# Cross attention on one core: cross scores as three fp32r products, zeros ahead of the first operands, halved first loads, finer PSUM claims, last stage by batch, a new merge

## The chip, the core and the metric

The kernel runs on one NeuronCore of a Trainium2 chip. A core has TensorE (matrix products, into the PSUM banks), VectorE, ScalarE, GpSimd and SyncE (here it only issues DMAs), each with an instruction stream of its own that runs in order; semaphores join them. The metric is the time of one execution on the device in microseconds, lower is better.

## What is computed

Two attention blocks over 8 batches of 112 tokens, width 256, 16 heads of 16. The first attends from x to the first 112 rows of a context under a causal mask and ends in a layer norm. The second is self attention, then cross attention to all 375 context rows, plus a feed-forward of width 1024 on the block's input:

```python
# block 0 (keys, values = context)
Q = relu(x @ Wq.T + bq); K = relu(ctx @ Wk.T + bk); V = relu(ctx @ Wv.T + bv)
x = layer_norm(softmax(mask(Q K^T / 4)) V + x) * gamma + beta
# block 1 (tgt = x, src = ctx)
q, k, v = split(ln1(tgt) @ sa_wqkv)
result = tgt + softmax(causal(q k^T / 16)) v @ sa_wproj + sa_bproj
k2, v2 = split(ln2(src) @ ed_wkv);  q2 = ln2(result) @ ed_wq
result = result + softmax(q2 k2^T / 16) v2 @ ed_wproj + ed_bproj
result = result + relu(ln3(tgt) @ ff_w1 + ff_b1) @ ff_w2 + ff_b2
```

## The kernel before

Batches go in four groups g of two (b = 0, 1). Heads are packed so that one product over 32 rows of the array serves two heads; four such products, for r = 0 to 3, use four row groups side by side (a "round" below). All work is cut into steps, and the steps are named by tuples: `("S", g, l, b)` is the self scores of layer l, needed only for their row maxima; `M` transposes and spreads the maxima; `X` makes the scores again, transposed and less their maximum (minus-max products with `sel`, then the scores), for ScalarE's exp; `V` sums values; `O` brings the sum back to token rows. The cross attention has the same steps: `cS` (four per batch, i = 0 to 3), `cM`, `cX` and `cV` (three chunks of 125 context rows each), `cO`; then `t2` transposes the result, `y` projects it, and the result is stored. `k2`, `v2`, `q2` are the cross projections, `cT` the transposed context; `h`, `f` the feed-forward; `q0`, `k0`, `v0`, `xT`, `q1`, `k1`, `v1`, `t1`, `proj`, `xqT` the projections and transposes of the self attention; `rows` spreads row vectors over partitions, `flag` and `general` handle fully masked rows.

The order of all steps is one string, `MIX`: each letter takes the next step of one stream (`STREAMS`), and every engine runs its part of each step in that order (`run`). TensorE writes into a ring of six PSUM banks, in three pairs. `homes` gives each job a pair, or one bank if its kind is in `SMALL`, the one filled longest ago; `claim` makes TensorE wait until the jobs that had it before have been read. A quad step (S, X, cS, cX) has two jobs, one for r = 0, 1 and one for r = 2, 3.

In `cross_scores` and `cross_shifted` the operands q2 and k2 are fp32, and each such matmul is recorded as two matmuls in the trace. The cross projections already work with split operands: an fp32 value is rounded to fp32r (HI), the rest is kept (LO), and three fp32r products, each recorded once, stand for one fp32 product:

```python
TERMS = ((HI, HI), (HI, LO), (LO, HI))
```

In the profile VectorE's reduction of cS is L1021, of S L1000, ScalarE's exp L848, its copy of k2 L901 and of q2 L829; `add_values` (V, cV) is L644, the minus-max products L619, cS L740, cX L754, X L631, S L593 and L599, most other products L493.

Of the kernel before, what the change touches and what calls it, by code (L numbers as in the profile page):

```python
# [7 lines left out]
F32 = mybir.dt.float32  # L8
# [12 lines left out]
G = 2  # L21
# [81 lines left out]
def b_steps(g, b):  # L103

    return [("cS", g, b, i) for i in range(4)] + [("cM", g, b), ("cX", g, b, 0), ("cX", g, b, 1), ("cV", g, b, 0), ("cX", g, b, 2), ("cV", g, b, 1), ("cV", g, b, 2), ("cO", g, b)]
# [9 lines left out]
           "F": [x for g in GROUPS for x in b_steps(g, 1)], "Y": [(n, g) for g in GROUPS for n in ("t2", "y")],  # L115
# [33 lines left out]
SMALL = ("counts", "M", "O", "cM", "cO", "f")  # L149
# [27 lines left out]
BEFORE = [(("rows", 0), ("v0", 0)), (("rows", 0), ("general",))]  # L177
for g_ in GROUPS:
    BEFORE += [(("keys", g_), ("v0", g_)), (("cV", g_, 0, 2), ("cV", g_, 1, 0))]
    for b_ in range(G):  # L180
        BEFORE += [(("keys", g_), ("S", g_, 0, b_)), (("masks", g_), ("M", g_, 0, b_)), (("late", g_), ("O", g_, 0, b_)), (("norm2", g_), ("f", g_, b_)), (("h", g_, 1), ("f", g_, b_)), (("f", g_, b_), ("y", g_)),
# [3 lines left out]
        if g_:  # L185
            BEFORE += [(("t2", g_ - 1), ("cO", g_, b_)), (("t1", g_ - 1), ("O", g_, 1, b_))]
# [4 lines left out]
    if g_:  # L191
        BEFORE += [(("h", g_ - 1, 1), ("xT", g_)), (("cV", g_ - 1, 1, 2), ("cV", g_, 0, 0)), (("proj", g_ - 1), ("t1", g_)), (("cT", g_ - 1, G - 1), ("stats", g_)),
                   (("t2", g_ - 1), ("t2", g_))]
# [15 lines left out]
def build(nc, xk_t_d, x_nat_d, keys_d, c_nat_d, c_t_d, c_first_d, mask_d, w_d, flat_d, mask_const_d, row_d, out_d):  # L209
    ctx = ExitStack()  # L210
    with ctx:
# [83 lines left out]
        unsplit = k2[1][:, :, :, :].rearrange("p b c s -> p (b c s)")[:, 0:C * 2 * U].rearrange("p (c u) -> p c u", c=C)  # L295
# [15 lines left out]
        PREP_DVE, PREP_LATE = 14, 2  # L311
        split_hi, split_lo = sem("weights_hi"), sem("weights_lo")
        prep_act = sem("prep_act"); prep_dve, prep_late = sem("prep_dve"), sem("prep_late"); prep_pool = sem("prep_pool")
        xk_loaded, x_loaded, stored = ([sem(f"{n}{i}") for i in range(2)] for n in ("xk_loaded", "x_loaded", "stored"))
# [7 lines left out]
        kv_loaded, qk0_loaded, v0_loaded = sem("kv_loaded"), sem("w_qk0_loaded"), sem("w_v0_loaded")  # L322
# [19 lines left out]
        a_ot = [twin("out_transposed0", 1), signal("out_transposed1", 1)]  # L342
        a_xq = twin("norm2_scaled", 2); a_q2 = twin("q2_scaled", 2); a_h = signal("hidden_biased", FF)
# [12 lines left out]
        v_res = signal("result", 1)  # L356
# [7 lines left out]
        def filled_and_taken(job):  # L364
# [7 lines left out]
                    "t1": lambda: (a_ot[0], 1), "proj": lambda: (v_proj, G), "xqT": lambda: (a_xq, 2), "q2": lambda: (a_q2, 2),  # L372
                    "h": lambda: (a_h, 4 * i[0] + 4), "cT": lambda: (v_ct, i[0] + 1), "k2": lambda: (a_k2, C * (i[0] + 1)), "shift": lambda: (a_shift, 2),
                    "v2": lambda: (v_v2, i[0] + 1), "cS": lambda: (x_max[i[0]], 2 * i[1] + i[2] + 1),
                    "cM": lambda: (c_m[i[0]], 1), "cX": lambda: (c_exp[i[0]], 2 * i[1] + i[2] + 1),
                    "cO": lambda: (x_o[i[0]], 2), "t2": lambda: (a_ot[1], 1), "y": lambda: (v_res, 1)}[kind]()
# [918 lines left out]
```

## Time and profile before

| | |
|---|---|
| three runs | 386.32, 382.94, 385.3 us (median 385.3) |
| the profiled execution | 384.1 us, span from first to last instruction 382.3 us |
| mean granted clock of TensorE | 0.995 |
| TensorE busy with matmuls | 341.8 us (89%), 4144 records |
| VectorE, ScalarE, GpSimd busy | 226.6, 172.5, 53.2 us |
| DMA | 13.43 MB, mean 35 GB/s |

The busy time of an engine is the union of its instructions. PE is TensorE's matmuls, PEld its weight loads, which run beside them; DVE is VectorE, ACT ScalarE, POOL GpSimd, SPq the DMA issues of SyncE. The difference between the execution's time and its span, 1.8 us, lies around the instructions.

### The profile page before, as it was taken

To read this page: it belongs to the slowest core of one execution; us is meant where nothing else is said; L and a number is where in the kernel's file an instruction comes from. 1 tells how busy PE (TensorE), PEld (TensorE's weight loads), DVE (VectorE), ACT (ScalarE), POOL (GpSimd) and SP (SyncE) were. 2 spreads that over 40 slices of the span, in tenths; PEclk is the share of its full clock that TensorE was granted. 3 is DMA by queue.
4 is the path that set the end of the run, shared out by engine and by line. 5 is a ranking of instruction groups with operands and counts; after the bars stand their busy time and mean duration, and the time that the engine had idled before them with its cause. 6 is when DMAs were issued, how large, how long until landed. Compare 5 with 4: busy or idle time off the path is not lost.

```text
span 382.3 us, 9700 instructions
## 1 busy us (share of the span) xinstructions
PE 341.8 (89%) x4144; PEld 261.7 (68%) x4144; DVE 226.6 (59%) x558; ACT 172.5 (45%) x297; POOL 53.2 (14%) x67
## 2 busy tenths in 40 slices
PE   7888699998999999998999999879989989887894
PEld 4666589886867777766668777655968757575663
DVE  5398997746657639564487545838943263645212
ACT  3346654465570263914326144655464535211551
POOL 2014141041320010120211012240100211000000
PEclk9999989999999999999999999999999999999999
DMA  7684103000000100000000020000000000000001
GB/s 223 186 328 137 63 2 104 3 2 2 25 2 0 45 40 24 3 2 2 24 6 3 0 82 2 3 0 26 3 2 2 2 2 2 3 0 0 3 2 48
DMA packets 4260, 13.43 MB, mean 35 GB/s; under 512 B 525, under 2 KB 1669, under 8 KB 3962
## 3 DMA queue, kind: packets, MB, share of 16 engines
q1 hardware_dynamic: 3928, 12.72, 10.0%
q8 instruction: 33, 0.54, 0.6%
q10 hardware_dynamic: 290, 0.10, 0.1%
q14 instruction: 9, 0.07, 0.1%
HBM read 11.89 MB, written 0.92 MB: 34 GB/s over the span
## 4 chain that ended last, share of the span: by engine, by line
PE 69%; DVE 16%; ACT 8%; issue 6%; ACTq 0%; DVEq 0%
PE ring L493 34%; PE ring L740 7%; DVE negmax L1021 7%; ACT exps L848 6%; PE ring L754 4%; PE ring L619 4%; PE ring L599 4%; PE ring L593 3%; PE acc L644 3%; PE ring L631 3%; DVE negmax L1000 3%; PE ring L663 2%; PE ring L611 1%; PE ring L705 1%; PE ring L525 1%
## 5 line engine op out<-in xcount | busy, mean ns | idle before, releaser
L1021 DVE TENSOR_REDUCE negmax<-ring 112x2 f32<-112x750 f32 x64 | 57.1, 936 | 42.2 <-PE ring L740 42.1
L848 ACT ACTIVATE exps<-ring 125x896 f32<-125x896 f32 x48 | 41.4, 914 | 43.7 <-PE ring L754 43.5
L1232 POOL TENSOR_SCALAR_AFFINE_SELECT exps<-exps 112x896 f32<-112x896 f32 x32 | 31.4, 1007 | 130.9 <-ACT exps L848 130.9
L1000 DVE TENSOR_REDUCE negmax<-ring 112x8 f32<-112x896 f32 x32 | 33.4, 1086 | 17.9 <-PE ring L599 17.7
L644 PE MATMUL acc<-exps,v 125*17 125x112 f32 (+1 forms) x1280 | 39.4, 264 | 0.8 <-ACT v L825 0.4
L644 PEld LDWEIGHTS acc<-exps,v 125*17 125x17 f32 (+1 forms) x1280 | 28.7, 98 | 13.8 <-issue 10.2
L848 ACT ACTIVATE exps<-ring,pad 112x896 f32<-112x896 f32 x32 | 30.5, 1004 | 16.7 <-PE ring L631 16.7
L740 PE MATMUL ring<-k,q 32*112 32x376 f32 x256 | 28.8, 517 | 10.2 <-DVE negmax L1021 6.0
L493 PE MATMUL ring<-w_b,h 128*112 128x256 f32 x128 | 29.5, 383 | 0.0
L619 PE MATMUL ring<-maxrows,sel 32*125 32x224 f32 (+1 forms) x320 | 19.1, 310 | 10.8 <-issue 2.9
L882 ACT ACTIVATE h<-ring,flat_c 128x224 f32<-128x224 f32 x32 | 11.7, 449 | 34.4 <-PE ring L493 34.4
L619 PEld LDWEIGHTS ring<-maxrows,sel 32*125 32x125 f32 (+1 forms) x320 | 12.3, 175 | 21.2 <-issue 13.7
L493 PEld LDWEIGHTS ring<-w_b,h 128*112 128x112 f32 x128 | 22.0, 177 | 6.6 <-issue 1.4
L493 PE MATMUL ring<-n,w_b 128*128 128x224 f32 x128 | 26.0, 357 | 0.1
L493 PEld LDWEIGHTS ring<-n,w_b 128*128 128x128 f32 x128 | 23.6, 190 | 1.6 <-issue 1.3
L740 PEld LDWEIGHTS ring<-k,q 32*112 32x112 f32 x256 | 9.9, 169 | 19.4 <-issue 19.1
L754 PE MATMUL ring<-q,k 32*125 32x224 f32 x384 | 22.7, 349 | 0.0
L493 PE MATMUL ring<-n,w_a 128*128 128x224 f32 x96 | 20.3, 360 | 0.2 <-ACT n L804 0.2
L493 PE MATMUL ring<-ct,wkv 128*128 128x376 f32 x96 | 18.4, 341 | 0.8 <-issue 0.7
L1217 POOL TENSOR_TENSOR rstd<-var_e,half 112x1 f32<-112x1 f32 x16 | 9.6, 603 | 67.8 <-DVE var_e L1113 51.2
L493 PEld LDWEIGHTS ring<-wkv,ct 128*125 128x125 f32 x144 | 17.6, 186 | 2.1 <-DVE negmax L1021 1.1
L493 PE MATMUL ring<-wkv,ct 128*125 128x256 f32 x144 | 19.1, 286 | 0.0
(143 smaller groups left out, 552.1 us busy)
## 6 DMA issues: line engine op xcount, KB each, us to landing
c_nat<-in_ctx SPq DMA_DIRECT2D x4, 750.0 KB
w_b<-in_w_b SPq DMA_DIRECT2D x1, 2304.0 KB, 10.2
xk_t<-in_xk_t SPq DMA_DIRECT2D x4, 448.0 KB, 4.1
w_a<-in_w_a SPq DMA_DIRECT2D x1, 1280.0 KB, 5.7
xh<-in_keys SPq DMA_DIRECT2D x4, 224.0 KB, 2.8
x_nat<-in_x SPq DMA_DIRECT2D x4, 224.0 KB, 4.0
out<-x SPq DMA_DIRECT2D x4, 224.0 KB, 2.4
w_qk<-in_w_qk SPq DMA_DIRECT2D x1, 512.0 KB, 4.7
```

Of the source, the lines that this page charges most:

```text
L493: m = nc.tensor.matmul(dst, lhs, rhs, start=start and n == 0, stop=n == len(pairs) - 1, skip_group_check=True)
L593: nc.tensor.matmul(bank[r][0:T, 0:4 * T], add_mask[:, l, slot(g, b), :], ident_b[:, :].unsqueeze(1).to_broadcast([T, 4, T]), start=True, s ...
L599: m = nc.tensor.matmul(bank[r][0:T, j * T:(j + 1) * T], qf[g % 2][32 * r:32 * r + 32, c, b, e, :], kf[g % 2][32 * r:32 * r + 32, c, b, :], ...
L619: nc.tensor.matmul(bank[r][0:k, 2 * c * T:2 * (c + 1) * T], sel[rows, c:c + 1].to_broadcast([32, k]), maxrows[i][rows, :], start=c == 0, s ...
L644: m = nc.tensor.matmul(acc[s][32 * p:32 * p + VW, 2 * c + m_, 0:T], vals(8 * c + 2 * r + e), exps[0:k, EXP_AT[job], rr, j * T:(j + 1) * T] ...
L740: m = nc.tensor.matmul(bank[r][0:T, 0:SP], q2[g % 2][rows, c, b, e, :], k2[g % 2][rows, b, c, :], start=True, stop=True)
L754: m = nc.tensor.matmul(bank[r][0:CH, 2 * c * T:2 * (c + 1) * T], k2[g % 2][rows, b, c, ch * CH:(ch + 1) * CH], q2[g % 2][rows, c, b, :, :] ...
L848: return nc.scalar.activation(exps[0:k, EXP_AT[job], :, :], o[0:k, :, 0:4 * T], ACT.Exp, bias=bias)
L882: a_h.step(nc.scalar.activation(h[g % 2][:, 4 * i0 + i, :, :].rearrange("p b t -> p (b t)"), o[:, i // 2, (i % 2) * G * T:(i % 2 + 1) * G ...
L1000: v_max[b].step(nc.vector.tensor_reduce(negmax[0][:, slot(g, b), 2 * m_:2 * m_ + 2, :], o[0:T, :, 0:4 * T].rearrange("p r (j t) -> p r j t ...
L1021: x_max[b].step(nc.vector.tensor_reduce(negmax[1][:, b, 2 * m_:2 * m_ + 2, i], o[0:T, :, 0:S], AX.X, ALU.max, negate=True), g, 2 * i + m_ + 1)
L1232: p_masked[b].step(nc.gpsimd.affine_select(e, e, [[0, 8], [1, T]], ALU.is_ge, 0.0, base=0, channel_multiplier=-1), g, k)
```

## The change

1. q2 and k2 are kept in two parts, HI and LO, as fp32r. ScalarE writes HI as it wrote the whole before; VectorE then computes the rest from the PSUM bank (`key2_rest`, `query2_rest`). cS and cX run the three `TERMS` instead of one fp32 product. cS and the release of k2's and q2's banks wait for VectorE.
2. `keep_busy`: TensorE multiplies zeros, ten bf16 products of 128x512, before its first step.
3. x's and the context's features, and the weights of q0 and k0, come by two loads each, with semaphores of their own; q0 waits for its own half.
4. `quad` claims its second pair of banks when it gets to r = 2. Masks and S wait for fewer of the mask steps.
5. `t2` and `y` go by batch, each in one bank, so do the copy, the residual add and the store; they belong to the streams B and F.
6. A new string `MIX`. `unsplit` (the cross weights as loaded) lies over h[1] instead of k2[1], and the DMA scratch is set to 1024.

```diff
-SMALL = ("counts", "M", "O", "cM", "cO", "f")
+SMALL = ("counts", "M", "O", "cM", "cO", "f", "t2", "y")
...
-MIX = ("RRLAANLNCNEDECDNCPAJCWNCWDEPIWDJINDPIJCIPDCDPIAJPAAIAJHJCJIHDEPCDPCEPEDCIDCDPJEAJIPAJAHAPINAAFIFJBPIJBKBABEPCHBNEBABPFBF"
+MIX = ("RALARLNNDENCAECDCNPJCNWCWDPIWDJICPDCJEIDNPDJPJAIAJAPDIJPHICHDCIAEPCEPEDPEIDPJCDCJIAJAIAPPAPAHFNIBHBBJBIJFKEBFEBAEPBBFABB"
...
-        q2 = [sb(f"q2_{i}", [128, C, G, 2, T]) for i in range(2)]
+        q2 = [sb(f"q2_{i}", [128, 2, C, G, 2, T], F32R) for i in range(2)]
...
-        k2 = [sb(f"k2_{i}", [128, G, C, SP]) for i in range(2)]
+        k2 = [sb(f"k2_{i}", [128, 2, G, C, SP], F32R) for i in range(2)]
...
-            load_x(0)
-            sp.dma_start(w_qk0[:, :, :, :].rearrange("p s c u -> p (s c u)"), w_d["qk0"]).then_inc(qk0_loaded, 16)
-            sp.wait_ge(xk_loaded[0], 16)
+            for part in range(2):
+                load_x(0, part)
+                sp.dma_start(w_qk0[:, part, :, :].rearrange("p c u -> p (c u)"), w_d["qk0"][:, part * C * U:(part + 1) * C * U]).then_inc((q0_loaded, k0_loaded)[part], 16)
+            sp.wait_ge(xq_loaded[0], 16)
...
-                pair = [claim(pe, step + (m,)) for m in range(2)]
-                return [pair[r // 2][:, r % 2, :] for r in range(R)]
+                pairs = {}
+
+                def bank(r):
+                    if r // 2 not in pairs:
+                        pairs[r // 2] = claim(pe, step + (r // 2,))
+                    return pairs[r // 2][:, r % 2, :]
+                return bank
...
-                pe.wait_ge(*a_q2.done(g))
-                pe.wait_ge(*a_k2.at(g, C * (b + 1)))
+                pe.wait_ge(*v_q2.done(g))
+                pe.wait_ge(*v_k2.at(g, C * (b + 1)))
                 bank = quad(("cS", g, b, i))
-                for r in range(R):
-                    rows = slice(32 * r, 32 * r + 32)
-                    m = nc.tensor.matmul(bank[r][0:T, 0:SP], q2[g % 2][rows, c, b, e, :], k2[g % 2][rows, b, c, :], start=True, stop=True)
-                    if r % 2:
-                        end(m)
+                for n, (qp, kp) in enumerate(TERMS):
+                    for r in range(R):
+                        rows = slice(32 * r, 32 * r + 32)
+                        m = nc.tensor.matmul(bank(r)[0:T, 0:SP], q2[g % 2][rows, qp, c, b, e, :], k2[g % 2][rows, kp, b, c, :], start=n == 0, stop=n == 2, skip_group_check=True)
+                        if n == 2 and r % 2:
+                            end(m)
...
+            def keep_busy(n):
+
+                for _ in range(n):
+                    nc.tensor.matmul(ring[2][:, 1, :], idle.bitcast(BF16)[:, 0:128], idle.bitcast(BF16), start=True, stop=True, skip_group_check=True)
+
+            pe.wait_ge(prep_dve, 1)
+            keep_busy(10)
...
+            def key2_rest(g, b):
+                o = is_filled(dve, ("k2", g, b))
+                dve.wait_ge(*a_k2.at(g, C * (b + 1)))
+                for i in range(C):
+                    hi, lo = (k2[g % 2][:, part, b, i, :] for part in (HI, LO))
+                    v_k2.step(nc.vector.scalar_tensor_tensor(lo, o[:, i, 0:SP], shift_k[:, i:i + 1], hi.bitcast(F32), ALU.add, ALU.subtract), g, C * b + i + 1)
+
+            def query2_rest(g):
+                o = is_filled(dve, ("q2", g))[:, :, 0:G * T].rearrange("p c (b t) -> p c b t", b=G)
+                dve.wait_ge(*a_q2.done(g))
+                for e in range(2):
+                    hi, lo = (q2[g % 2][:, part, :, :, e, :] for part in (HI, LO))
+                    v_q2.step(nc.vector.scalar_tensor_tensor(lo, o, eo_scale[:, 1, e:e + 1], hi.bitcast(F32), ALU.mult, ALU.subtract), g, e + 1)
```

How the order changes is shown at three places, all on TensorE. A row is a line of the kernel, what it writes and reads, the shape of the output and the number of matmuls as written (an fp32 one is two records in the trace).

The first is the start, up to the first self scores. Before, with rows (L560 to the second L493), flag (L569), q0 and k0 (L493, eight), masks, S (L593, L599):

```order
L560 MATMUL ring<-exps,ones_row 125x256
L562 MATMUL ring<-exps,ones_row 112x512
L563 MATMUL ring<-exps,ones_row 112x256
L493 MATMUL ring<-exps,ones_row 112x256 x2
L569 MATMUL acc<-ones,first_masked 1x1
L493 MATMUL ring<-xk_t,w_qk 128x224 x8
```

And after, with the zeros in the first row (L818):

```order
L818 MATMUL ring<-acc_sb 128x512 x10
L578 MATMUL ring<-exps,ones_row 125x256
L504 MATMUL ring<-xk_t,w_qk 128x224 x4
L587 MATMUL acc<-ones,first_masked 1x1
L504 MATMUL ring<-xk_t,w_qk 128x224 x4
L580 MATMUL ring<-exps,ones_row 112x512
L581 MATMUL ring<-exps,ones_row 112x256
L504 MATMUL ring<-exps,ones_row 112x256 x2
```

q0 moved ahead of the flag, and the second part of rows behind k0.

The second is the last cross key projection (k2(3,1), L504 with ct and wkv) and what follows it, after; before, it stands far ahead of its first cS:

```order
L504 MATMUL ring<-ct,wkv 128x376 x12
L637 MATMUL ring<-maxrows,sel 125x224 x8
L774 MATMUL ring<-q_1,k_1 125x224 x24
L759 MATMUL ring<-k_1,q_1 112x376 x24
L662 MATMUL acc<-exps,v_1 17x112 x16
```

One cX (L637, L774) stands between k2(3,1) and the two cS that read it (L759).

The third is the end, from the last cX on. Before:

```order
L619 MATMUL ring<-maxrows,sel 125x224 x8
L754 MATMUL ring<-q_1,k_1 125x224 x8
L644 MATMUL acc<-exps,v_1 17x112 x32
L663 MATMUL ring<-flat_c,acc_sb 112x128 x4
L493 MATMUL ring<-w_b,o_t 112x256 x4
L525 MATMUL ring<-flat_c,o_nat 128x112 x4
L493 MATMUL ring<-w_b,o_t 112x256 x4
```

And after:

```order
L637 MATMUL ring<-maxrows,sel 125x224 x8
L774 MATMUL ring<-q_1,k_1 125x224 x24
L662 MATMUL acc<-exps,v_1 17x112 x16
L801 MATMUL ring<-flat_c,o_nat 128x112 x2
L662 MATMUL acc<-exps,v_1 17x112 x16
L681 MATMUL ring<-flat_c,acc_sb 112x128 x4
L504 MATMUL ring<-w_b,o_t 112x256 x2
L801 MATMUL ring<-flat_c,o_nat 128x112 x2
L504 MATMUL ring<-w_b,o_t 112x256 x2
```

The y of group 2 is gone from between cO (L663, now L681) and the transposes (L525, now L801), and t2 and y of batch 0 of group 3 stand ahead of those of batch 1.

## Rows read from the trace of the kernel before

**Rows 1.** The page, part 1: busy time of TensorE (PE) and the others.

```profile
PE 341.8 (89%) x4144; PEld 261.7 (68%) x4144; DVE 226.6 (59%) x558; ACT 172.5 (45%) x297; POOL 53.2 (14%) x67
```

**Rows 2.** Stretches: from:to, length, busy us of PE, PEld, DVE, ACT, POOL, then clock.

```profile
0.00:20.00 20.00, 16.11 (x86) 11.64 (x90) 9.10 (x40) 7.26 (x15) 2.08 (x7) 1.00 0.66 201
40.00:50.00 10.00, 7.07 (x114) 5.43 (x110) 9.21 (x27) 5.42 (x11) 2.88 (x4) 0.85 0.09 23
50.00:350.00 300.00, 277.17 (x3341) 214.57 (x3334) 182.55 (x427) 137.47 (x239) 42.08 (x51) 1.00 0.04 13
350.00:380.00 30.00, 24.05 (x382) 17.16 (x380) 7.54 (x14) 10.95 (x15) 0.00 (x0) 1.00 0.03 9
```

**Rows 3.** The page, part 4: the chain that ended last.

```profile
PE 69%; DVE 16%; ACT 8%; issue 6%; ACTq 0%; DVEq 0%
```

**Rows 4.** Timeline of the start (start us, length us, engine, line, tiles, idle before).

```profile
3.37 1.91 PE L562 MATMUL ring<-exps,ones_row 1*112 1x512 f32 x2
...
5.99 0.31 SPq L419 DMA_DIRECT2D x_nat<-in_x  x1
...
7.88 1.02 ACT L811 ACTIVATE rows_sb<-ring 112x1024 f32<-112x1024 f32 x1 [0.35 <-PE ring L493]
7.94 5.71 PE L493 MATMUL ring<-xk_t,w_qk 128*128 128x224 f32 x16
...
14.67 0.94 PE L593 MATMUL ring<-mask_c,add_mask 112*112 112x448 bf16 x4 [0.97 <-ACT kf L804]
```

**Rows 5.** Groups of products in 57.4 to 60 us (count, busy us, mean ns).

```profile
L493 PE MATMUL ring<-n,w_a 128*128 128x224 f32 x15 | 3.0, 353 | 0.0
```

**Rows 6.** Timeline of TensorE from 47 to 50.5 us.

```profile
47.08 1.76 PE L631 MATMUL ring<-qf,kf 32*112 32x224 f32 x16
48.77 1.70 PE L644 MATMUL acc<-exps,v 112*17 112x112 f32 x32
```

**Rows 7.** Timeline of TensorE: a cS step and the step behind it.

```profile
190.88 0.90 PE L740 MATMUL ring<-k,q 32*112 32x376 f32 x8 [0.22 <-DVE negmax L1021]
191.72 0.54 PE L663 MATMUL ring<-flat_c,acc_sb 128*112 128x128 f32 x3
```

**Rows 8.** Timeline from 191.47 to 191.7 us: only the cS step's second round runs.

```profile
191.26 0.52 PE L740 MATMUL ring<-k,q 32*112 32x376 f32 x4
```

**Rows 9.** Timeline from 357.565 to 357.6 us: two rounds run.

```profile
357.36 0.31 PE L619 MATMUL ring<-maxrows,sel 32*125 32x224 f32 x4
357.48 0.39 PE L754 MATMUL ring<-q,k 32*125 32x224 f32 x4
```

**Rows 10.** Timeline of TensorE: a cX step and the step behind it.

```profile
353.17 0.96 PE L754 MATMUL ring<-q,k 32*125 32x224 f32 x16
354.06 0.96 PE L644 MATMUL acc<-exps,v 125*17 125x112 f32 x32
```

**Rows 11.** Timeline of TensorE: fp32r products over the whole array.

```profile
76.19 2.37 PE L493 MATMUL ring<-wkv,ct 128*125 128x256 f32 x18
78.49 0.47 PE L619 MATMUL ring<-maxrows,sel 32*112 32x224 f32 x8
```

**Rows 12.** VectorE's nearest form (count, busy us, mean ns, idle before).

```profile
L1164 DVE SCALAR_TENSOR_TENSOR wkv<-k,flat_c,wkv 128x512 fp32r<-128x512 f32 x2 | 1.5, 742 | 0.0
```

**Rows 13.** Weight loads of the cX products (count, busy us, mean ns).

```profile
L754 PEld LDWEIGHTS ring<-q,k 32*125 32x125 f32 x384 | 16.7, 183 | 0.0
```

**Rows 14.** Timeline of the end.

```profile
373.83 1.89 PE L493 MATMUL ring<-w_b,o_t 128*112 128x256 f32 x8
374.33 0.42 DVE L1095 TENSOR_TENSOR o_nat<-ring,sums 112x256 f32<-112x256 f32 x1
...
375.56 0.55 PE L525 MATMUL ring<-flat_c,o_nat 112*128 112x112 f32 x4
...
376.74 1.98 PE L493 MATMUL ring<-w_b,o_t 128*112 128x256 f32 x8 [0.64 <-ACT o_t L869]
378.76 0.69 DVE L1160 TENSOR_TENSOR x<-ring,x 112x512 f32<-112x512 f32 x1 [2.31 <-PE ring L493]
```

More of the change, by code:

```diff
@@ L618, in minus_max @@
                         rows = slice(32 * r, 32 * r + 32)
-                        nc.tensor.matmul(bank[r][0:k, 2 * c * T:2 * (c + 1) * T], sel[rows, c:c + 1].to_broadcast([32, k]), maxrows[i][rows, :], start=c == 0, stop=False, skip_group_check=True)
+                        nc.tensor.matmul(bank(r)[0:k, 2 * c * T:2 * (c + 1) * T], sel[rows, c:c + 1].to_broadcast([32, k]), maxrows[i][rows, :], start=c == 0, stop=False, skip_group_check=True)
             def self_max_rows(g, l, b):
@@ L751, in cross_shifted @@
                 for c in range(C):
-                    for r in range(R):
-                        rows = slice(32 * r, 32 * r + 32)
-                        m = nc.tensor.matmul(bank[r][0:CH, 2 * c * T:2 * (c + 1) * T], k2[g % 2][rows, b, c, ch * CH:(ch + 1) * CH],
-                                             q2[g % 2][rows, c, b, :, :].rearrange("p e t -> p (e t)"), start=False, stop=True, skip_group_check=True)
-                        if c == C - 1 and r % 2:
-                            end(m)
+                    for n, (qp, kp) in enumerate(TERMS):
+                        for r in range(R):
+                            rows = slice(32 * r, 32 * r + 32)
+                            m = nc.tensor.matmul(bank(r)[0:CH, 2 * c * T:2 * (c + 1) * T], k2[g % 2][rows, kp, b, c, ch * CH:(ch + 1) * CH],
+                                                 q2[g % 2][rows, qp, c, b, :, :].rearrange("p e t -> p (e t)"), start=False, stop=n == 2, skip_group_check=True)
+                            if c == C - 1 and n == 2 and r % 2:
+                                end(m)
             def cross_sum(g, b, ch):
@@ L775, in cross_out, with out2_transposed @@
                 tokens_first(o, RING["cO", g, b])
-            def out2_transposed(g):
-                rows_transposed(("t2", g), o_nat[1], lambda b: pe.wait_ge(*x_o[b].done(g)))
+            def out2_transposed(g, b):
+                o = claim(pe, ("t2", g, b))
+                pe.wait_ge(*x_o[b].done(g))
+                for c in range(C):
+                    m = nc.tensor.transpose(o[:, 0, c * T:(c + 1) * T], o_nat[1][:, b, c * 128:(c + 1) * 128], ident[0:T, 0:T])
+                end(m)
             def hidden_out(g, b):
@@ L1154, in add_hidden, with result @@
                 v_f[b].step(nc.vector.tensor_tensor(x1[g % 2][:, b, :], o[0:T, 0, 0:U], x1[g % 2][:, b, :], ALU.add), g, 1)
-            def result(g):
-                o = is_filled(dve, ("y", g))
-                for b in range(G):
-                    dve.wait_ge(*v_f[b].done(g))
-                v_res.step(nc.vector.tensor_tensor(x1[g % 2][:, :, :], o[0:T, :, 0:U], x1[g % 2][:, :, :], ALU.add), g, 1)
+            def result(g, b):
+                o = is_filled(dve, ("y", g, b))
+                dve.wait_ge(*v_f[b].done(g))
+                v_res[b].step(nc.vector.tensor_tensor(x1[g % 2][:, b, :], o[0:T, 0, 0:U], x1[g % 2][:, b, :], ALU.add), g, 1)
             def weights_lo(i):
```

118 lines of the change are left out of this document (66 added, 52 removed).

## The prediction

> **What bounds the kernel now.** I read the page's busy times first: TensorE has matmuls in flight for 341.8 of 382.3 us, VectorE works 226.6, ScalarE 172.5 [rows 1]. Then the same by stretch: TensorE lacks 3.9 us in the first 20, 2.9 in 40 to 50, 22.8 in the 300 us from 50 to 350, and 6.0 in the last 30 [rows 2]. The reader is to see that the middle is nearly full, and that holes of several per cent stand only at both ends and around 45 us. The chain that ended last says the same: 69% TensorE, 16% VectorE, 8% ScalarE, 6% issue [rows 3]. So work taken off TensorE counts nearly in full, work added to VectorE counts only where TensorE has nothing else queued, and the ends are read by timeline.
>
> **The sum** is made against the profiled execution, 384.1 us (span 382.3). The median of three runs is 385.3, so 384.1 stands 0.3% below it; a forecast from it may be low by 1.2. About 1% is what a measurement of this kernel can tell from no change.
>
> **Cross scores in three fp32r products.** There are 32 steps cS and 24 steps cX. A cS step is recorded as 8 matmuls, in two rounds of four that run side by side on four row groups. It starts at 190.88, its second round at 191.26, the next step at 191.72: 0.84 us [rows 7, 8]. Whole-array fp32 matmuls of 224 columns stand 3.0/15 = 0.20, nearer 0.19 without the last one's drain, apart [rows 5]; by columns that is 0.32 for 376, so 0.84 is two rounds of 0.32 and 0.20 of starting and handing over. A cX step has four rounds of 0.19 and 0.13 on top: 353.17 to 354.06, 0.89 [rows 10]. Afterwards cS has three rounds and cX six, each of single-record matmuls. What does such a round cost? Eighteen fp32r products of 256 columns over the whole array take 76.19 to 78.49, 2.30, less the same 0.20 for the handing over 0.117 each [rows 11]: 0.17 for 376 columns. For 224 columns on row groups, the second fp32r round of the minus-max products and the first behind it stand 0.12 apart in rounded figures [rows 9]; 256 columns cost 0.117, so I take 0.11. cS: 3 x 0.17 + 0.20 = 0.71, 0.13 less, x32 = -4.2. cX: 6 x 0.11 + 0.13 = 0.79, 0.10 less, x24 = -2.4. **Together -6.6.** Lower end: a fp32r round costs half a fp32 one (0.16 and 0.095), 0.16 and 0.19 less a step, -9.7. Upper end: no round is shorter than the weight load recorded for it, 0.183 [rows 13]; cS 0.75 and cX 1.23, -2.9 and +8.2, +5.3. I take the inner value because those 0.12 and 0.117 are such rounds, weight loads included.
>
> The Trainium skill (TensorE: Matmul & The Clock Gate, Part 3, Packing small matmuls) says that a weight load overlaps a matmul in flight only when it is for another row group, and its section on LDWEIGHTS prices a load at P/1.2 ns, 104 ns for the 125 columns of cX. By that rule cX would go, as an estimate, from 4 x (104 + 187) to 6 x (104 + 93) ns, no gain, and cS from 2 x (93 + 313) to 3 x (93 + 157) ns; the sum would be some 5 us later. The trace speaks against it: eighteen products that each load all rows anew stand 0.117 apart [rows 11], where load and product one after the other would be 0.21.
>
> **The rests on VectorE.** Splitting k2 adds 16 scalar_tensor_tensor of 376 columns, q2 adds 8 of 448. The nearest row is 742 ns for 512 columns [rows 12]; by columns 0.55 and 0.65, 8.8 + 5.2 = 14.0 us. Two instructions each make twelve groups that stand in VectorE's queue with ScalarE's copy ahead of them. They hold a pair of banks 1.1 or 1.3 us longer, and cS waits for them instead of for ScalarE; behind them in VectorE's queue are the maxima that free the ring. Where other work lies between k2 and its first cS this is hidden. In the new order it isn't for the last one, k2(3,1), which has one cX between (0.79 and its minus-max products), about as long as ScalarE's copy: VectorE's 1.1 us are bare. I take two such places of twelve, **+2.5**; the ends are 0 and 14.0.
>
> **The start.** Before, the one-row products fill 3.37 to 7.8, q0 and k0 take 7.94 to 13.65, and the first S begins at 14.67 [rows 4]. q0 and k0 run there at 5.71/16 = 0.357 a matmul against 0.20 later [rows 4, 5]: TensorE is at the lower of its two levels (1.2 against 2.4 GHz), though one-row products had kept it busy for over 4 us. (The profile's clock column has 1.00 for the first 20 us [rows 2]; I go by the products.) Afterwards ten zero products of 512 columns come first: at the lower level 0.357 x 512/448 = 0.41 each, from about 1.2 us to 5.3. rows(0) takes half of the 1.91 of rows 4, to 6.2; q0's operands are there by 5.99 even unhalved (the load that waits for the second one is issued then); q0 1.5 at the upper level, to 7.7; the flag still waits for its own chain until 7.8; k0 to 9.4; rows(1), 4.5 before, 2.3 at the upper level, to 11.7. ScalarE's copy of rows(1), 1.02, frees the second pair of S at 12.7, while the finer claim lets the first pair start at 11.7. So 14.67 becomes 11.7 to 12.7, **-2.3**. The halving is worth nothing here, because the flag holds k0; if the flag's cover goes, q0's earlier operands would be worth up to 1.5. Ends: +0 (the zeros don't raise the clock) and -3.5.
>
> The page of the skill named above (Part 1) says that the array is throttled by default and that activity releases it. The trace agrees in the pair 0.357 and 0.20, but the busy one-row stretch did not release it, so busy time alone isn't it; all-zero products are shown by no run here.
>
> **The dip at 47 us.** The granted clock of 40 to 50 is 0.85; the X step's second half at 47.08 takes 1.76 and the one behind it 1.70, where such steps take 0.96 [rows 2, 6, 10]: 1.5 us. Ahead of them TensorE idles most of its 2.9 us. The new merge puts v0(1), 1.7 us of products, among these steps, and k2(0,0) ahead of the V. I take **-1.0** of the 1.5; ends 0 and -2.5.
>
> **The end.** In the last 9 us: y(2) of both batches stands between the cross output and its transposes, which start at 375.56 although o_nat is ready at 374.75 (0.8); then transposes 0.55, copy, y 1.98 for both batches, result 0.69, store [rows 14]. By batch, half of each remains: transposes 0.3, y 1.1, result 0.45, and y(3,0) fits into the wait ahead. 0.8 + 0.25 + 0.9 + 0.25 and 0.1 on ScalarE's copy: **-2.3**; ends -1.5 and -3.0. Splitting all eight t2 and y adds about 0.2 to an instruction on ScalarE and VectorE, hidden in the middle. Twice as many stores and first loads cost SyncE issue time, with nobody waiting for it.
>
> **The new merge otherwise: 0.** It can only move the 22.8 us of holes. Thin covers are there in both orders: t1 straight behind the last O, cO behind its cV. A quarter of the holes either way is 5.7.
>
> **Sum:** 384.1 - 6.6 + 2.5 - 2.3 - 1.0 - 2.3 = **374.4**.
>
> **Rivals.**
> (a) The merge closes a quarter of the middle's holes: 368.7. For it: banks come in smaller pieces, t2 and y take one bank each, a quad claims its second pair later. Against: k2 and q2 hold theirs longer.
> (b) It opens as much: 380.1. For it: steps cS stand in twos and threes in the order with two maxima each on VectorE, which holds 16% of the chain [rows 3].
> (c) The zeros don't raise the clock, and the start stays as it was: 376.7.
> (d) VectorE's rests all lie on the path: 14.0 for 2.5, 385.9. For it: they queue ahead of maxima. Against: VectorE idles 155 us.
> (e) Slower than before: weight loads bound the short rounds. Every row-group round costs 0.183 [rows 13], so that cX gets 0.34 longer: +5.3 for -6.6, 386.3. The point is a round of 0.174 in both steps, where the whole change comes to nothing. This is the place of the rule of the skill quoted above (weight loads hidden only behind other row groups). Against it stand the 0.12 and 0.117.
>
> **Chances.** Forecast 0.48, (a) 0.17, (b) 0.12, (c) 0.08, (d) 0.09, (e) 0.06. The range goes from 367 to 384: it leaves out (d), (e) and a deeper (a), 0.2. Faster by over 1% (below 381.4) holds the forecast, (a), (c) and most of (b): 0.82. Within 1%: 0.14. Slower: 0.04.
>
> **What would show it.** cS to the next step 0.71 and cX 0.79 when nothing waits; 24 more VectorE instructions, 14 us; q0's and k0's matmuls 0.19 to 0.2 apart, the first S at 11.7 to 12.7; a clock of 1.00 in 40 to 50; from the y product ahead of the last transposes to the end of the span 6.2 us instead of 8.5 (373.83 to 382.3). The prediction fails if rounds of row groups stand over 0.15 apart, if TensorE's waits for k2's and q2's rests exceed 5 us, or if its idle time between 50 and 350 us changes by over 6.

## The result, and the profile after

The changed kernel takes 375.06 us (median of four runs, 370.83 to 377.79) against 385.77 for the one before: a ratio of 0.966, 95% interval 0.956 to 0.976. Medians are over all runs, but each ratio here and below leaves out the runs in a second, slower state with a lower granted clock, here two of the four (376.59 and 377.79 us), so it can lie below the quotient of the medians. Run again beside other kernels it took 374.64 (0.975, 0.9705 to 0.9795). The forecast was 374.4. That the number came out does not mean that its sum did: as the experiments show, its terms of together -9.7 us bring about nothing, and the edit that carries the whole gain had no term. The number is right by luck.

The page of the changed kernel, first and fourth part (busy time; the chain that ended last), answers to [rows 1, 3]:

```profile
span 371.7 us, 10386 instructions
PE 343.2 (92%) x4474; PEld 270.2 (73%) x4474; DVE 237.8 (64%) x587; ACT 172.9 (47%) x301; POOL 52.9 (14%) x67
PE 63%; DVE 26%; issue 4%; ACT 3%; POOL 0%; DVEq 0%; ACTq 0%
```

TensorE is busy as long as before; what shrank is its idle time, span less busy time: 28.5 us instead of 40.5. VectorE gained 11 us of work, and 10 points of the chain. The same stretches as in [rows 2]:

```profile
0.00:20.00 20.00, 17.60 (x124) 10.77 (x125) 10.58 (x43) 7.32 (x15) 2.08 (x7) 1.00 0.70 193
40.00:50.00 10.00, 10.00 (x119) 8.18 (x120) 9.13 (x27) 5.81 (x8) 5.64 (x7) 1.00 0.15 48
50.00:350.00 300.00, 282.17 (x3679) 226.48 (x3677) 195.21 (x447) 138.32 (x241) 38.96 (x47) 0.99 0.04 14
350.00:380.00 30.00, 17.27 (x329) 13.04 (x327) 3.88 (x10) 8.74 (x13) 0.00 (x0) 0.95 0.03 10
```

The hole around 45 us is closed in this profile (in that of `after_again` 1.4 us of it are there, and the clock is down), and the middle lacks 17.8 us instead of 22.8. The timeline of TensorE after, of the start, of two cS steps, of a cX step and of the end, answers to [rows 4, 7, 10, 14]:

```profile
1.26 4.35 PE L818 MATMUL ring<-acc_sb 128*128 128x512 bf16 x10 [1.26 <-DVE acc_sb L1214]
6.17 1.78 PE L504 MATMUL ring<-xk_t,w_qk 128*128 128x224 f32 x8
8.62 1.77 PE L504 MATMUL ring<-xk_t,w_qk 128*128 128x224 f32 x8
12.78 0.56 PE L611 MATMUL ring<-mask_c,add_mask 112*112 112x448 bf16 x2
13.84 0.59 PE L611 MATMUL ring<-mask_c,add_mask 112*112 112x448 bf16 x2 [0.50 <-ACT rows_sb L843]
...
108.00 0.77 PE L759 MATMUL ring<-k,q 32*112 32x376 f32 x12
108.70 0.96 PE L662 MATMUL acc<-exps,v 112*17 112x112 f32 x32
...
188.28 0.85 PE L774 MATMUL ring<-q,k 32*125 32x224 f32 x24
189.06 0.96 PE L662 MATMUL acc<-exps,v 125*17 125x112 f32 x32
...
365.59 1.03 PE L504 MATMUL ring<-w_b,o_t 128*112 128x256 f32 x4
366.65 0.38 PE L801 MATMUL ring<-flat_c,o_nat 112*128 112x112 f32 x2
367.57 1.09 PE L504 MATMUL ring<-w_b,o_t 128*112 128x256 f32 x4 [0.54 <-ACT o_t L904]
```

A cS step takes 0.70 to the step behind it (forecast 0.71), a cX step 0.78 (0.79). The groups of the cS products, of the minus-max products and of the rests (count, busy, mean ns, idle time ahead of them) show what was bought and what was paid:

```profile
L759 PE MATMUL ring<-k,q 32*112 32x376 f32 x384 | 29.3, 376 | 4.4 <-DVE k L1183 1.9 <-DVE negmax L1056 1.6 <-ACT h L917 0.8
L637 PE MATMUL ring<-maxrows,sel 32*125 32x224 f32 (+1 forms) x320 | 22.3, 317 | 2.7 <-DVE k L1183 1.7 <-DVE q L1190 0.7 <-DVE x L1090 0.2
L1183 DVE SCALAR_TENSOR_TENSOR k<-ring,shift_k,k 128x376 fp32r<-128x376 f32 x16 | 9.0, 603 | 7.7 <-PE ring L774 6.1 <-PE ring L649 1.6
L1190 DVE SCALAR_TENSOR_TENSOR q<-ring,eo_scale,q 128x448 fp32r<-128x448 f32 x8 | 5.1, 679 | 14.5 <-ACT q L861 10.6 <-PE ring L649 3.8
```

The same two groups of matmuls before, from the trace that the prediction had, but not among its rows:

```profile
L740 PE MATMUL ring<-k,q 32*112 32x376 f32 x256 | 28.8, 517 | 10.2 <-DVE negmax L1021 6.0 <-ACT exps L848 3.6 <-ACT qf L818 0.4
L619 PE MATMUL ring<-maxrows,sel 32*125 32x224 f32 (+1 forms) x320 | 19.1, 310 | 10.8 <-issue 2.9 <-DVE negmax L1021 2.6 <-DVE ct L1141 1.6
```

21.0 us of idle time ahead of two kinds of products, half of all that TensorE idles, and 7.1 after. The prediction makes no use of this pair of rows.

### The profile page after: what moved, and what is told of

Same layout as the page of the kernel before. It is cut to its first block, busy times and chain, and to the rows that moved or that the text cites. A ratio compares the mean times of both kernels' runs of the same rounds, so it can differ in the third digit from the quotient of the medians.

```text
span 371.7 us, 10386 instructions
## 1 busy us (share of the span) xinstructions
PE 343.2 (92%) x4474; PEld 270.2 (73%) x4474; DVE 237.8 (64%) x587; ACT 172.9 (47%) x301; POOL 52.9 (14%) x67
## 4 chain that ended last, share of the span: by engine, by line
PE 63%; DVE 26%; issue 4%; ACT 3%; POOL 0%; DVEq 0%; ACTq 0%
PE ring L504 34%; DVE negmax L1056 8%; PE acc L662 5%; PE ring L759 4%; PE ring L637 4%; DVE negmax L1035 4%; PE ring L617 3%; PE ring L774 3%; PE ring L611 3%; PE ring L649 2%; DVE k L1183 2%; PE ring L629 2%; PE ring L681 1%; DVE v L1198 1%; PE ring L723 1%
## 5 line engine op out<-in xcount | busy, mean ns | idle before, releaser
L1056 DVE TENSOR_REDUCE negmax<-ring 112x2 f32<-112x750 f32 x64 | 56.2, 934 | 13.3 <-PE ring L759 13.0
L662 PE MATMUL acc<-exps,v 125*17 125x112 f32 (+1 forms) x1280 | 40.2, 265 | 0.1
L880 ACT ACTIVATE exps<-ring,pad 112x896 f32<-112x896 f32 x32 | 30.5, 1004 | 11.3 <-PE ring L649 11.1
L759 PE MATMUL ring<-k,q 32*112 32x376 f32 x384 | 29.3, 376 | 4.4 <-DVE k L1183 1.9
L504 PE MATMUL ring<-w_b,h 128*112 128x256 f32 x128 | 29.4, 383 | 0.0
L759 PEld LDWEIGHTS ring<-k,q 32*112 32x112 f32 x384 | 17.7, 178 | 13.0 <-issue 9.7
L504 PE MATMUL ring<-n,w_b 128*128 128x224 f32 x128 | 25.8, 356 | 0.4 <-DVE negmax L1056 0.3
L504 PEld LDWEIGHTS ring<-w_b,h 128*112 128x112 f32 x128 | 22.1, 177 | 5.3 <-issue 0.6
L504 PEld LDWEIGHTS ring<-n,w_b 128*128 128x128 f32 x128 | 23.8, 190 | 1.5 <-issue 1.4
L637 PE MATMUL ring<-maxrows,sel 32*125 32x224 f32 (+1 forms) x320 | 22.3, 317 | 2.7 <-DVE k L1183 1.7
L637 PEld LDWEIGHTS ring<-maxrows,sel 32*125 32x125 f32 (+1 forms) x320 | 14.3, 175 | 12.2 <-issue 10.6
L917 ACT ACTIVATE h<-ring,flat_c 128x224 f32<-128x224 f32 x32 | 11.7, 449 | 22.3 <-PE ring L504 22.3
L504 PE MATMUL ring<-n,w_a 128*128 128x224 f32 x96 | 20.2, 360 | 0.6 <-DVE v L1198 0.3
L774 PE MATMUL ring<-q,k 32*125 32x224 f32 x576 | 20.6, 267 | 0.0
L611 PE MATMUL ring<-mask_c,add_mask 112*112 112x448 bf16 x64 | 16.6, 364 | 3.1 <-ACT exps L880 1.3
L504 PE MATMUL ring<-wkv,ct 128*125 128x256 f32 x144 | 19.2, 287 | 0.2 <-ACT exps L880 0.2
L504 PEld LDWEIGHTS ring<-n,w_a 128*128 128x128 f32 x96 | 17.5, 190 | 2.3 <-issue 2.1
L504 PE MATMUL ring<-ct,wkv 128*128 128x376 f32 x96 | 18.6, 342 | 0.4 <-issue 0.4
```

Source lines behind the costliest of these rows:

```text
L504: m = nc.tensor.matmul(dst, lhs, rhs, start=start and n == 0, stop=n == len(pairs) - 1, skip_group_check=True)
L611: nc.tensor.matmul(bank(r)[0:T, 0:4 * T], add_mask[:, l, slot(g, b), :], ident_b[:, :].unsqueeze(1).to_broadcast([T, 4, T]), start=True, s ...
L637: nc.tensor.matmul(bank(r)[0:k, 2 * c * T:2 * (c + 1) * T], sel[rows, c:c + 1].to_broadcast([32, k]), maxrows[i][rows, :], start=c == 0, s ...
L662: m = nc.tensor.matmul(acc[s][32 * p:32 * p + VW, 2 * c + m_, 0:T], vals(8 * c + 2 * r + e), exps[0:k, EXP_AT[job], rr, j * T:(j + 1) * T] ...
L759: m = nc.tensor.matmul(bank(r)[0:T, 0:SP], q2[g % 2][rows, qp, c, b, e, :], k2[g % 2][rows, kp, b, c, :], start=n == 0, stop=n == 2, skip_ ...
L774: m = nc.tensor.matmul(bank(r)[0:CH, 2 * c * T:2 * (c + 1) * T], k2[g % 2][rows, kp, b, c, ch * CH:(ch + 1) * CH], q2[g % 2][rows, qp, c, ...
```

## Experiments

Three groups of four kernels were run, each group beside the kernel before, whose median was 384.8, 385.0 and 385.3. Each ratio compares with the runs of its own group. Edits are shown abbreviated.

**Each part alone or taken out.** In the first group, `terms_only` is the kernel before with the products and the rests (and, as they need it, `unsplit` over h[1] and the smaller DMA scratch):

```
-    for r in range(R):  m = matmul(bank[r], q2[rows, c, b, e], k2[rows, b, c])
+    for n, (qp, kp) in enumerate(TERMS):
+        for r in range(R):  m = matmul(bank[r], q2[rows, qp, c, b, e], k2[rows, kp, b, c], start=n == 0, stop=n == 2)
+    "k2": key2_rest, "q2": query2_rest      # on VectorE; PE's waits for a_k2, a_q2 become v_k2, v_q2
```

> The kernel before with one part of the change alone: k2 and q2 in two parts, cS and cX as three fp32r products, the rests on VectorE; merge, loads, claims and last stage as before. Theory A (the terms of the prediction add up): -6.6 for the products, and for the rests +2.5 or somewhat more, because the old merge leaves them less room: 4 us less than before, ratio 0.99, cS steps 0.70 long and cX 0.75 to 0.79 where nothing waits. Rival B (products and rests cancel, and the gain of the whole change is the merge's): within 1 us of before. Rival C (rests all on the path): 5 us or more slower.

Measured: 406.48 us, 1.054 (1.051 to 1.058). Far slower, though the products did shrink.

`old_merge` is the changed kernel with the order of before (each Y written twice, since t2 and y go by batch):

> The changed kernel with the letters of the old merge; t2 and y stay by batch, both batches of each standing where the pair stood, so y(2) is again between the last cO and the last t2. Theory A: the merge is worth the dip at 47 us (1.0), the place of rows and q0 in the start (most of 2.3) and y(2) at the end (0.8), so 377 to 379 on the scale on which the changed kernel has 374, and TensorE's idle time between 50 and 350 us up by less than 3 us. Rival B (the merge carries the gain): 382 to 386, with the idle time of the middle up by 7 or more.

Measured: 396.61, 1.033 (1.029 to 1.036).

`claims_whole` is the changed kernel with one line more in `quad`:

```
+                bank(0), bank(2)
                 return bank
```

> The changed kernel where a quad step claims both pairs of banks before its first product, as before the change. In the trace of the changed kernel some quad steps start early and then stand still in mid-step, their first two row groups alone. Theory A: the finer claim is worth 0 to 2 us (only the first round of a step goes ahead). Rival: the split rounds cost what they bring, and whole claims are as fast or 1 us faster.

Measured: 387.84, 1.005 (1.002 to 1.008): the whole gain is gone with this one line.

`no_zeros` is the changed kernel without `keep_busy(10)`:

> The changed kernel without the ten zero products. Theory A: q0 and k0 start at the lower clock, their matmuls 0.36 to 0.37 apart, first S 1.5 to 3 us later than the 12.8 of the changed kernel, the whole 1.5 to 2.5 us slower. Rival: the start has slack (flag, copies), q0's eight slow products hide in it and the whole loses less than 0.7 us.

Measured: 374.73, 0.974 (0.970 to 0.978): no difference. Without the zeros q0 runs at the lower clock, but starts as soon as its operands land, at 4.40 instead of 6.17, and the first scores stand at 13.27 instead of 12.78. In this profile the clock falls again at 14.5 us, 1.3 us behind the one-row products.

**Where the 21 us of the terms come from.** The timeline of `terms_only` around one of three waits of its kind:

```profile
81.09 2.28 PE L494 MATMUL ring<-ct,wkv 128*128 128x376 f32 x12 [0.69 <-issue]
83.41 1.04 ACT L904 ACTIVATE k<-ring,shift_k 128x376 fp32r<-128x376 f32 x2 [1.15 <-PE ring L494]
84.55 1.13 DVE L1151 SCALAR_TENSOR_TENSOR k<-ring,shift_k,k 128x376 fp32r<-128x376 f32 x2 [2.56 <-ACT k L904]
85.59 0.17 DVE L1007 CAST spread<-negmax 112x16 fp32r<-112x16 f32 x1
85.80 0.19 DVE L1009 TENSOR_TENSOR spread<-negmax,spread 112x16 fp32r<-112x16 f32 x1
...
86.13 0.96 PE L612 MATMUL ring<-ident_r,spread 112*128 112x112 f32 x4 [2.76 <-DVE spread L1009]
```

The spread needs only maxima that are long there. It stands in VectorE's queue behind the rest, the rest behind ScalarE's copy, the copy behind TensorE's k2, and M behind the spread: TensorE waits for its own product to go round three engines. Over the whole run TensorE idles 17.7 us more than before (58.2 for 40.5). By the idle columns 7.5 of them are direct waits for a rest (4.4 for k2's, 3.1 for q2's), and 8.5 are waits for steps queued behind one (5.4 more for spreads, 3.1 for the norm's output xh). The next two experiments take this apart. `terms_late` moves four of the eight k2 rests behind the steps that follow them directly:

```
+            for step in [s for s in ORDER if s[0] == "k2"]:
+                i = out.index(step)
+                while out[i + 1][0] in ("M", "cM", "dev", "norm"):
+                    out[i], out[i + 1] = out[i + 1], out[i]
+                    i += 1
-            for kind, *rest in ORDER:           # VectorE alone
+            for kind, *rest in out:
```

> The kernel before with the three-term products and the rests alone (406.5 us, 5.4% slower than before), and one difference: on VectorE the rest of a k2 goes behind the deviations, norms and spreads that stand directly behind it in the order (k2(0,0), k2(0,1), k2(2,1), k2(3,0)). Nothing else moves, and no work is left out. In the profile without this PE waits 2.74 us at 60.26 for the norm, 2.76 at 86.13 and 2.76 at 242.68 for the spread, each behind a rest that itself waited for the copy of k2, and each followed by some 3.5 us at half the clock. Theory (the rest's place in VectorE's queue is the cost): the three waits fall under 1 us, which gives some 2 us each, and the three dips go, 1.7 us each: 11 us less, 395 to 397. Rival 1 (the rests' own busy time of 14 us is what costs, wherever they stand): under 3 us less, 404 or more. Rival 2 (the waits go, the clock dips stay, since they come from something else): 6 us less, 400 to 401.

Measured: 396.61, 1.030 (1.026 to 1.034), 9.9 us less, near the theory's 11; one new wait, of 3.90 us, stands ahead of v2 at 286.48, where the rest that moved back now comes too late. What is left of the 21 us is mostly the direct wait: TensorE idles 12.4 us more than before (52.9), 9.5 of it for the rests themselves. `terms_filled` leaves the queue alone and only keeps TensorE at work in the waits:

```
                 o = claim(pe, job)
+                fill(o[:, 0, :], 10 if job in (("M", 0, 1, 0), ("M", 2, 1, 0)) else 0)   # and in front of xT(0)
                 pe.wait_ge(*made)
```

> The kernel before with the three-term products and the rests alone (406.5 us), VectorE's order untouched, and ten all-zero bf16 products of 128x512 (0.215 us each at the upper clock, 2.15 in sum) on PE in front of the same three waits of 2.7 us (xT(0), M(0,1,0), M(2,1,0)), into the bank that is claimed anyway and written over afterwards. The waits stay as long as they are. Theory (the lower clock follows from PE standing idle, and each dip costs some 1.7 us): the granted clock stays at 1.0 after 62, 86 and 242 us, the dips elsewhere (44, 170, 276, 300, 356) stay, and the kernel takes 5 us less, 401 to 402. Rival (the dips have another cause, or zeros do not count as work): the dips stay and the time is 406 to 407, or more where the zeros outlast the wait.

Measured: 399.16, 1.035 (1.031 to 1.039), 7.3 us less. The dips are seen in stretches behind the wait, of `terms_only`, `terms_late` and `terms_filled` in this order (granted clock third from the end):

```profile
86.00:90.00 4.00, 3.87 (x19) 3.88 (x20) 0.26 (x2) 0.72 (x2) 0.00 (x0) 0.57 0.02 4
```

```profile
80.00:84.00 4.00, 4.00 (x40) 3.56 (x39) 3.72 (x14) 2.63 (x4) 1.55 (x2) 1.00 0.02 4
```

```profile
86.00:92.00 6.00, 6.00 (x69) 4.94 (x68) 4.12 (x14) 3.50 (x5) 3.10 (x3) 1.00 0.00 0
```

Apart from one small memset, zeros changed nothing but what TensorE did while it waited, and the clock stayed up at these three places. Not all of the 7.3 us is theirs. The profile of `terms_only` has eight stretches at the lower level, seven of 3.4 us and one, near 45 us, of 6.8; that of `terms_filled` has three of 3.4. The three behind the filled waits are gone, but so are half of the one near 45 and those at 277 and 356, where nothing was filled. Three stretches of 3.4 us at half speed make an estimate of 5 us for the three waits, as the theory had it; the rest of the 7.3 came with stretches elsewhere. The two repairs overlap, so their worths don't add. Over the whole span the page's row of the granted clock shows it coarsely (40 slices; first `terms_only`, then `terms_filled`):

```profile
PEclk9999798989999999989999998998989999989999
```

```profile
PEclk9999999999999999999999999999989999999999
```

**Terms against claims against merge.** `fp32_scores` is the changed kernel with the fp32 cS and cX of before and no rests, `fp32_whole` the same with whole claims, and `claims_only` the kernel before with nothing but the `quad` of the changed one.

> The changed kernel with the cross scores and the shifted cross scores again as single fp32 products, and so without the rests on VectorE and the waits for them; the new merge, the finer claims, the zeros, the halved loads and the last stage by batch stay. Theory 1 (the terms of the prediction, as the trace after has them): the shorter products are worth 6.6 us, the waits for the rests cost 4.3 us, so without both the kernel takes 2 us more, 377, with its clock as before. Theory 2 (the rests also cost clock: the two stretches at the lower level, after 160 and after 338 us, both follow waits for a rest and go with them, some 3.3 us more): the kernel takes 374, a tie. Rival (the new merge is fitted to the three-term products and is a poor order for fp32): 380 or more, with new waits on PE of over 5 us.

Measured: 375.21, 0.973 (0.970 to 0.977). Beside it `after_again`:

> The changed kernel itself, run beside the other three of this group on one chip, so that they can be compared with it. Expected: 375 us within 1%, a ratio of 0.96 to 0.975.

> The kernel before with one edit: a step of scores claims its two pairs of banks one after the other, each where its first product needs it, in place of both ahead of the first product. Products, order, loads and last stage are those of before. Theory 1 (finer claims are worth as much in any order: taking them back out of the changed kernel cost 12.7 us): 373 to 375, a ratio of 0.97. Theory 2 (their worth belongs to the three-term steps and the rests, which hold the banks longer): 383 to 385, a tie, with PE's waits for negmax (7.1 us there with whole claims) as they are in before. Theory 3, as the prediction had it: no worth outside the start, a tie as well; theories 2 and 3 are told apart by the next kernel.

Measured: **375.39, 0.975 (0.972 to 0.978)**. One edit of six lines gives what the whole change gives.

> The changed kernel with single fp32 products for the cross scores, no rests, and whole claims: what is left of the change is the new merge, the zeros, the halved loads and the last stage by batch. With finer claims the same kernel takes 375.2 us. Theory 1 (finer claims are worth 12 us here too, and the new merge leans on them): 387, a tie with before or slower. Theory 2 (they are worth that only where rests hold the banks): 376 to 378, so that the new merge alone carries nearly the whole gain.

Measured: 388.39, 1.010 (1.006 to 1.013). Theory 1 holds for both. The eight combinations, in us (the column of the new merge also has the zeros, the halved loads and the last stage by batch, as has the cell marked *):

| products | claims | old merge | new merge |
|---|---|---|---|
| fp32 | whole | 385.3 | 388.4 |
| fp32 | finer | 375.4 | 375.2 |
| three terms | whole | 406.5 | 387.8 |
| three terms | finer | 396.6 * | 374.6 to 375.1 |

Read down, finer claims are worth 10 to 13 us in every column. Read across, the new merge costs 3 or nothing with fp32 products and is worth 19 to 22 with the terms. The terms cost 21 in the old merge and nothing in the new one. The page of `claims_only` (busy times, then the same two groups as above) shows where the 10 us lie:

```profile
span 373.0 us, 9660 instructions
PE 349.2 (94%) x4144; PEld 267.2 (72%) x4144; DVE 225.9 (61%) x558; ACT 172.0 (46%) x297; POOL 52.7 (14%) x67
L745 PE MATMUL ring<-k,q 32*112 32x376 f32 x256 | 35.0, 519 | 1.1 <-DVE negmax L1026 0.4
L624 PE MATMUL ring<-maxrows,sel 32*125 32x224 f32 (+1 forms) x320 | 24.2, 320 | 3.6 <-DVE negmax L1026 2.4
```

Idle time ahead of the two groups fell from 21.0 to 4.7 us, and all of TensorE's from 40.5 to 23.8. Of these 16.7 us 7.4 came back as busy time (349.2 for 341.8; these two groups have 11.3 more): the halves of a step now often run apart, and half a step is recorded as long as a whole one (0.89 us for the four records at 329.22, 0.90 for eight before). The span is 9.3 us shorter. One place, in the timeline of the kernel before and then of `claims_only`:

```profile
326.62 0.90 PE L740 MATMUL ring<-k,q 32*112 32x376 f32 x8 [0.21 <-ACT exps L848]
327.55 1.79 DVE L1021 TENSOR_REDUCE negmax<-ring 112x2 f32<-112x750 f32 x2 [7.31 <-PE ring L740]
328.63 0.90 PE L740 MATMUL ring<-k,q 32*112 32x376 f32 x8 [0.22 <-DVE negmax L1021]
329.56 1.79 DVE L1021 TENSOR_REDUCE negmax<-ring 112x2 f32<-112x750 f32 x2 [0.23 <-PE ring L740]
330.64 0.90 PE L740 MATMUL ring<-k,q 32*112 32x376 f32 x8 [1.11 <-DVE negmax L1021]
331.48 0.65 PE L663 MATMUL ring<-flat_c,acc_sb 128*112 128x128 f32 x4
331.57 1.79 DVE L1021 TENSOR_REDUCE negmax<-ring 112x2 f32<-112x750 f32 x2 [0.23 <-PE ring L740]
```

```profile
318.58 1.08 PE L745 MATMUL ring<-k,q 32*112 32x376 f32 x8
319.51 5.38 DVE L1026 TENSOR_REDUCE negmax<-ring 112x2 f32<-112x750 f32 x6 [6.92 <-PE ring L745]
320.48 2.82 PE L745 MATMUL ring<-k,q 32*112 32x376 f32 x16
323.26 0.65 PE L668 MATMUL ring<-flat_c,acc_sb 128*112 128x128 f32 x4
```

The ring has three pairs of banks and a step takes two. With whole claims a step waits until VectorE has read a pair of the step before, while the third pair stands free and empty: the second and third step start 2.01 us apart, and VectorE idles 0.23 ahead of each. With finer claims the free pair is filled meanwhile, and VectorE reduces six times with no idle time between: 5.38 us where the six took 5.81 before (327.55 to 333.36). The waits of 0.22 and 1.11 us that vanish are not what is won, since the second half of a step still waits for VectorE: from the second step to the product behind the third it is 2.78 us for 2.85, and from the first step 4.68 for 4.86. The gain comes in such small pieces. Both kernels issue the same products in the same order, and the same value sums start at the same time at 84 us, 2.1 us earlier at 167, 4.9 at 252, 7.8 at 325 and 9.1 at 370. The Trainium skill (Perfetto Trace Analysis, Optimization Strategy) says that the same gap repeating on the engine that should be saturated can mean too little SBUF or PSUM for the next tile. The trace of the kernel before agrees as to the place: 1.11, 1.12 and 1.23 us ahead of the step behind a cS, at 330.64, 337.53 and 352.88. With the same number of banks most of this idle time went once fewer were asked for at a time; more banks were not tried.

**Two smaller questions.** `unhalved` loads x, keys and the first weights whole:

> The changed kernel with x and keys of a group, and the two first weights, loaded whole again: q0 waits for both transfers instead of for two halves. The prediction put the halving at nothing, because the flag and the rows hold the first scores. In the profile after, q0 begins at 6.17 us, the rows' products end at 12.7 and the first scores start at 12.78 behind the copies of the rows. Theory 1 (halving is worth nothing): 375, the first scores at 12.8. Theory 2 (q0 is late by the time of half the transfer, about 1 us, and the whole head moves with it, since PE is busy from q0 to the first scores with no wait over 0.6 us): 376, first scores at 13.8.

Measured: 374.46, 0.963 (0.958 to 0.968). q0 starts at 6.00 behind a wait of 0.16 for its weights, the first scores at 12.07: the halving brings nothing, as predicted. Its ratio is even below that of `after_again` from another group (0.975) and near that of the first result (0.966), so that a small cost of the halving is not excluded. `after_filled` puts zeros in front of three waits of the changed kernel:

> The changed kernel with all-zero bf16 products of 128x512 (0.215 us each) in front of three of PE's longest waits: six before the sums' transpose at 39.95 (wait 1.41), six before the M at 91.51 (1.55) and four before the first cS of group 3, batch 1 at 337.93 (1.39), there into the second pair of banks, claimed first. Theory (the clock falls after such waits: in one profile of this kernel at 162 and 340 us, in another of the same kernel at 14 and 42 us, some 3.5 us at half clock each): the dips at 42 and 340 no longer occur, those at 14 and 162 still may, and the kernel takes 1 to 2 us less, 373 to 374. Rival (a wait of this length mostly leaves the clock alone, since most of them in these profiles are not followed by a dip, and the zeros delay what follows by what they outlast): 375 or 376.

Measured: 373.16, 0.969 (0.966 to 0.972), against 0.975 (0.9705 to 0.9795) for `after_again` from another group. The intervals touch, so a gain of 1 to 2 us is likely and not settled. It is the lowest median of all kernels here, but no version is clearly better than the changed one.

## Why the prediction was right, and where it wasn't

**The products, -6.6: right by the step.** 0.70 and 0.78 for 0.71 and 0.79. Rival (e), weight loads as the bound, is out: the loads of cX are still recorded at 184 ns, and six rounds of them fit into a step of 0.78. The Trainium skill (TensorE: Matmul & The Clock Gate, Part 3, Packing small matmuls) lets a load overlap only a matmul of another row group, which with the load price of its section LDWEIGHTS makes an estimate of 6 x (104 + 93) ns = 1.18 us for such a step, load and product one after the other; the 0.78 measured speak against it.

**The rests, +2.5: mis-sized.** Their own time was right (9.0 + 5.1 us for 14.0 forecast). TensorE's waits for them are 4.8 us over all groups, just inside the limit of 5 that the prediction set itself, but the kernel without terms and rests takes 375.2 and with both 374.6: they eat up the 6.6 almost whole. From `fp32_scores` to after TensorE's idle time rises from 21.0 (374.6 less 353.6) to 28.5 us, 7.5 where the step had 2.5. Of these 4.8 are its own waits for rests, at six places and not two, and 1.3 are longer waits for spreads (4.8 us for 3.5). What the step missed: it gave a rest its own time at two places, and took "behind them in VectorE's queue are the maxima" for covered. Neither the wait of a rest for its copy nor the steps queued behind it have a price in it; in the old order these steps cost more than the direct waits (8.5 for 7.5). The named place, k2(3,1), was right, with 1.39 us of wait for 1.1, and a second one of 0.85 behind it.

**"The new merge otherwise: 0": wrong in the form in which it was put.** The two orders are not alike. In the old one, four k2 stand directly ahead of spreads or norms; with the terms the old order costs 22 us more than the new one (396.6 for 374.6). With fp32 products the merge does bring nothing, as the step said (375.2 for 375.4 with finer claims; with whole ones it costs 3). So the term is right for the kernel that was before and wrong for the one that it was added to: it was weighed without the rests, and the rests were weighed in the new order alone.

**Finer claims: no term, and 10 of the 10 us.** The prediction gave them only "the finer claim lets the first pair start at 11.7" and a half-sentence in rival (a), at 0.17. This is the step that failed: the forecast counts the middle's 22.8 us of holes as unchanged. In rival (a) a quarter of them closes, 5.7 us; in `claims_only` TensorE's idle time from 50 to 350 us falls to 9.5, in `fp32_scores` to 11.0. In the changed kernel it is back at 17.8, since the rests put their waits there; so the change of 5.0 stayed inside the limit of 6 at which the prediction would have called itself wrong. Without the finer claims the whole change takes 387.8 (`claims_whole`), 13 us above the forecast. That the sum came within 1 us is luck.

**The start, -2.3: 1.9 measured, but not by the zeros.** The first scores came at 12.78 for 14.67, and the clock was up from q0 on, so rival (c) is out as put; without the zeros they come at 13.27, so that most of it is the new order of q0, k0 and the rows. Nothing of it shows in the median.

**The dip, -1.0.** It is gone in the first profile, which has two others, at 162 and 340 us; the second profile of the same kernel has them at 15 and 42. Where a dip falls is not fixed by the program alone. **The end, -2.3: right.** From the y product ahead of the last t2 (365.59) to the end of the span 6.1 us, for 6.2 forecast.

All in all: finer claims -10, and the terms, the rests, the merge, the start, the dip and the end together about 0, where the sum had -9.7 for these and 0 for the claims. `claims_only` and `fp32_scores` differ by merge, start and end, forecast at 4.6 to 5.6 us, and tie (375.4 and 375.2). Where that went is only partly open to view: TensorE's idle time is 2.8 us less (21.0 for 23.8), its busy time 4.4 more, and the zeros are 4.35 us of busy time at the lower clock; more dips in the one profile are likely the rest. One profile of each is too little to settle it.

## What to carry to other kernels

Before costing what an edit adds, price every part of the diff from the idle column of the groups that it touches: 21 us stood there, ahead of the very products whose claims were changed. Idle time ahead of a product is not all to be won, though: of 16.7 us that vanished 9.3 came off the span. Instructions added to an in-order queue cost what waits for them and what stands behind them while they wait themselves, not what they take; list for each what its queue neighbours feed. And never add terms that were weighed in different orders: 21 us of cost and 22 us of cure cancelled here.

## What the runs showed of the hardware

- The granted clock of TensorE fell to its lower level (1.2 of 2.4 GHz), mostly for some 3.4 us, behind waits of 0.8 to 2.8 us (0.76 at 162 us in `after`, 2.76 at 86 in `terms_only`), but not behind all of them, and at other places in a second profile of the same kernel. All-zero bf16 products in the wait kept it up at three places of three in `terms_filled`.
- All-zero products raised the clock at the start: q0's matmuls stand 0.22 us apart behind them (1.78 for 8) and 0.42 without (3.36 for 8), where products of one row had run ahead of them. Behind the one-row products that follow q0 and k0 it fell again in three profiles with the zeros (`after_again` at 15.2 us, `fp32_scores` and `after_filled` at 13.1 to 13.2) and stayed up in two (`after`, `unhalved`); what decides this is not shown.
- In fp32 half a cS step (four records on two row groups) takes as long as a whole one (eight on four): 0.89 us in `claims_only`, 0.90 before.
- fp32r products are recorded once, fp32 ones twice. On row groups, rounds of 224 columns stand 0.11 us apart, with loads recorded at 184 ns each.
